# One-hot scatter on TensorE: a window of 12 destinations in groups of eight chunks, every source one-hot on VectorE

## The reference

```python
batch0 = jnp.zeros((512,), jnp.int32)
x = x + _L0_gnn_ref(_layernorm(x), batch0, edge_index, edge_attr_16, ...)[0]
x = x + _L0_ffn_ref(_layernorm(x)[None], ...)[0]
x = x + _L1_gnn_ref(_layernorm(x), edge_index, edge_weight, ...)
x = x + _L1_ffn_ref(_layernorm(x)[None], ...)[0]

# in _L0_gnn_ref: 32 graphs of 16 nodes, 8 heads, attention inside each graph
eb = edge_attr @ We + be
attn = attn.at[b_idx, loc_src, loc_dst].add(eb)     # a bias for each edge, summed where edges repeat
attn = jax.nn.softmax(attn, axis=2)
# in _L1_gnn_ref: Chebyshev terms over the weighted adjacency
deg = jax.ops.segment_sum(edge_weight, row, num_segments=n)
out = jax.ops.segment_sum(norm_w[:, None] * h[row], col, num_segments=n)
```

## Time and profile before

| | |
|---|---|
| median of 3 runs | 804.68 us (804.19 to 804.76) |
| the profiled execution | 805.79 us, its span from first to last instruction 804.0 us |
| busy: PE, PEld | 675.7 us (84%), 566.8 us (70%) |
| busy: DVE, ACT, POOL | 589.9 us (73%), 462.0 us (57%), 119.1 us (15%) |
| granted TensorE clock, mean | 0.93 |
| chain that ended last | PE 60%, DVE 20%, issue 7%, DMA 5% |

### The profile page before, as it was taken

How to read it: one execution, slowest core, us unless ns; L and a number is a source line. 1 busy time by engine, 2 the same in 40 slices (tenths; PEclk the granted TensorE clock), 3 DMA queues, 4 the chain that set the end, 5 groups by cost and what they waited for, 6 DMA issues and landing times.

```text
span 804.0 us, 23192 instructions
## 1 busy us (share of the span) xinstructions
PE 675.7 (84%) x8392; PEld 566.8 (70%) x8393; DVE 589.9 (73%) x1220; ACT 462.0 (57%) x804; POOL 119.1 (15%) x175
## 2 busy tenths in 40 slices
PE   2995888866659899999997099999669999999991
PEld 1454788854349899999987054444368999999991
DVE  4658988864469898888896673345578888888881
ACT  3360888862146687777765361111247888878780
POOL 2000000002000022112222200000000324433233
PEclk9897999996959999999999589999879999999996
DMA  9504000000105888989883850000117888889764
GB/s 305 213 1 158 0 0 0 0 1 1 67 3 192 300 280 270 327 285 339 288 265 86 264 197 2 1 0 1 69 58 246 262 256 269 257 269 281 254 199 86
DMA packets 37775, 127.67 MB, mean 159 GB/s; under 512 B 5441, under 2 KB 6033, under 8 KB 37569
## 3 DMA queue, kind: packets, MB, share of 16 engines
q1 hardware_dynamic: 31712, 119.39, 42.8%
q0 software_dynamic: 3648, 6.23, 5.3%
q10 hardware_dynamic: 2352, 1.23, 0.7%
HBM read 117.85 MB, written 10.03 MB: 159 GB/s over the span
## 4 chain that ended last, share of the span: by engine, by line
PE 60%; DVE 20%; issue 7%; DMA 5%; ACT 2%; POOL 2%; ACTq 1%; DVEq 1%; SPq 0%; POOLq 0%
PE pb L1473 11%; PE pb L1474 11%; PE pb L1475 11%; PE pb L1696 5%; DMA r_stage<-in_chunks 5%; PE pb L1572 4%; DVE r_split L952 4%; PE pb L1727 3%; PE pb L1729 3%; PE pb L1728 3%; DVE r_work L1073 2%; PE pb L1482 2%; ACT r_split L681 1%; PE pb L1570 1%; DVE r_work L1065 1%
## 5 line engine op out<-in xcount | busy, mean ns | idle before, releaser
L952 DVE SCALAR_TENSOR_TENSOR r_split<-r_stage,r_split 128x1024 f16<-128x1024 f32 (+1 forms) x160 | 230.3, 1443 | 47.3 <-ACT r_split L681 46.8
L681 ACT ACTIVATE r_split<-r_stage 128x1024 f16<-128x1024 f32 (+1 forms) x160 | 197.3, 1237 | 49.5 <-PE pb L1729 31.3
L1473 PE MATMUL pb<-r_work,r_split 128*128 128x160 f16 x864 | 184.0, 234 | 6.9 <-DVE r_work L1333 5.1
L1474 PE MATMUL pb<-r_work,r_split 128*128 128x160 f16 x864 | 184.0, 234 | 0.0
L1475 PE MATMUL pb<-r_work,r_split 128*128 128x160 f16 x864 | 184.0, 234 | 0.0
L1727 PE MATMUL pb<-r_work,r_split 128*128 128x160 f16 x608 | 129.9, 233 | 5.4 <-ACT r_work L779 3.2
L1729 PE MATMUL pb<-r_work,r_split 128*128 128x160 f16 x608 | 129.9, 233 | 0.0
L1728 PE MATMUL pb<-r_work,r_split 128*128 128x160 f16 x608 | 129.9, 233 | 0.0
L1570 PE MATMUL pb<-r_work 128*128 128x64 f16 x512 | 87.9, 195 | 11.6 <-DVE r_work L1073 11.6
L1473 PEld LDWEIGHTS pb<-r_work,r_split 128*128 128x128 f16 x864 | 84.9, 98 | 8.6 <-issue 7.1
L1572 PE MATMUL pb<-r_work 128*128 128x256 f16 x512 | 89.7, 276 | 0.0
(11 more groups left out here) (283 smaller groups left out, 1331.7 us busy)
## 6 DMA issues: line engine op xcount, KB each, us to landing
r_stage<-in_chunks SPq DMA_DIRECT2D x68, 768.0 KB, 5.2
r_stage<-in_chunks SPq DMA_DIRECT2D x92, 512.0 KB, 4.9
r_gnn<-in_cheb_lin SPq DMA_DIRECT2D x3, 1024.0 KB, 8.8
r_split<-in_cheb_lin SPq DMA_DIRECT2D x3, 1024.0 KB, 12.0
x_dram<-x_sb SPq DMA_DIRECT2D x10, 256.0 KB, 2.7
x_sb<-in_x SPq DMA_DIRECT2D x1, 1024.0 KB, 5.7
r_split<-in_Wq SPq DMA_DIRECT2D x1, 1024.0 KB, 9.8
r_work<-in_attr SPq DMA_DIRECT2D x1, 1024.0 KB, 11.2
```

What stands on the lines that cost most here:

```text
L681: nc.scalar.activation(x.hi(c), x.stage(c), ACT.Copy, scale=W_SCALE).then_inc(x.whi, 1)
L952: V.scalar_tensor_tensor(x.lo(c), x.stage(c), W_SCALE, x.hi(c), ALU.mult, ALU.subtract)\
L1473: MM(o, sh, mh, start=start, stop=False)
L1474: MM(o, sh, ml, start=False, stop=False)
```

## The change

The window falls from 64 to 12 destinations, and the edge bias uses the same window: one matmul of 2 x 12 x 8 = 192 columns, written at a register's column. The place in the graph of 16 is the destination's low four bits; a window that starts at place e covers places e to e + 11, past 15 too, so each tile block has a whole bank of two halves (high, low) of 256 columns, and the halves are folded afterwards by a reduction over the four groups of 128 columns. The second register of a chunk (`ends`) is the low bits of its first destination times 8. Buffers hold NC = 8 chunks instead of 4; the loop has 8 iterations of two buffers, and each buffer loads its own 8 + 8 registers. All source one-hots are made by DVE and none by ACT. The one-column closing matmuls take the place of the 512-column ones, over eight banks. Four reductions and one update replace the four updates behind the scatter. `weight_lo` of chunks 0 to 3 leaves its place ahead of the scores: two stand behind DVE's one-hots, two inside the attention loop, at t = 1 and t = 2. `dl_hot` is made in the wide path alone. The wide path keeps buffers of four.

```diff
-    W = 64
+    W = 12
-        score_m = [view(r_work, 8 + b, ...) for b in range(2)]
+        score_m = [view(r_work, 26 + b, ...) for b in range(2)]
+        NC = 8
...
-            V.tensor_scalar(src_neg[:, :], pb[0][:, 0:C], -1.0, None, ALU.mult)
             ch.link(V.tensor_scalar(w_lo[:, :], pb[0][:, 3 * P:3 * P + C], EDGE_SCALE, None, ALU.mult))
-            V.tensor_copy(base_i[:, :], pb[1][0:1, 0:C])
+            ch.link(V.tensor_copy(firsts_i[:, 0, :], pb[1][0:1, 0:C]))
+            ch.link(V.tensor_scalar(firsts_i[:, 1, :], firsts_i[:, 0, :], GN - 1, None, ALU.bitwise_and))
+            ch.link(V.tensor_scalar(firsts_i[:, 1, :], firsts_i[:, 1, :], float(H), None, ALU.mult))
...
-            for c in range(AHEAD):
-                weight_lo(ex[0], 0, c)
-
             dve.wait_ge(score_psum, T)
...
+            def hots_narrow(i, b, free):
+                if free:
+                    dve.wait_ge(hot_used, i * 2 + (b - 1))
+                at = bass.ds(i * (2 * NC) + b * NC, NC)
+                V.tensor_tensor(rel_hot[b], bc(iota_n[:, 0:W], 1, NC), bc(rel_h[:, at], 2, W), ALU.is_equal)\
+                    .then_inc(rel_ready, 1)
+                for c in range(NC):
+                    one = bass.ds(i * (2 * NC) + (b * NC + c), 1)
+                    V.tensor_scalar(src_hot_n[b][:, c, :], iota_n[:, :], src_f[:, one], None, ALU.is_equal)
+                dve.wait_ge(rel_ready, i * 2 + (b + 1))
+                for s, w in enumerate((w_h16, w_l16)):
+                    V.tensor_tensor(dst_n[b][:, :, s, :], rel_hot[b], bc(w[:, at], 2, W), ALU.mult)
+                for s, eb in enumerate((eb_hi, eb_lo)):
+                    last = V.tensor_tensor(ebd_n[b][:, :, s, :].rearrange("p c (g h) -> p c g h", h=H),
+                                           bc(rel_hot[b], 3, H), bc(eb[:, at, :], 2, W), ALU.mult)
+                last.then_inc(hot_ready, 1)
...
+            for c in range(2):
+                weight_lo(ex[0], 0, c)
             dve.wait_ge(scatter_psum, 1)
             flat = score.rearrange("p t k h -> p t (k h)")
-            for s in range(2):
-                for i in range(2):
-                    ins = V.scalar_tensor_tensor(...)
-                    ch.link(ins)
+            for t in range(T):
+                ch.link(V.tensor_reduce(eb_sum[:, t, :], pb[4 + t][:, :].rearrange("p (x q) -> p q x", x=4), AX_X,
+                                        ALU.add))
+            ch.link(V.scalar_tensor_tensor(flat, eb_sum, 1.0 / EB_SCALE, flat, ALU.mult, ALU.add))
...
                 if 1 <= t <= T:
                     head_lo(t - 1)
+                if 1 <= t <= 2:
+                    weight_lo(ex[0], 0, t + 1)
                 if t >= 2:
                     project(t - 2)
...
+            def scatter_narrow(i, b):
+                firsts, ends = [nc.values_load_multi_w_load_instructions(
+                    firsts_i[0:1, s, bass.ds(i * (2 * NC) + b * NC, NC)], engines=[mybir.EngineType.PE], min_val=0,
+                    max_val=top, skip_runtime_bounds_check_because=why)[1]
+                    for s, top, why in (...)]
                 pe.wait_ge(hot_ready, i * 2 + (b + 1))
-                pe.wait_ge(hot_act, i * (2 * AC) + (b + 1) * AC)
+                for c in range(NC):
+                    cols, near = bass.ds(firsts[c], W), bass.ds(ends[c], W * H)
+                    for t in range(T):
+                        w = src_hot_n[b][:, c, t * P:(t + 1) * P]
+                        MM(pb[t][:, cols], w, dst_n[b][:, c, 0, :], start=False, stop=False, skip_group_check=True)
+                        MM(pb[t][:, cols], w, dst_n[b][:, c, 1, :], start=False, stop=False, skip_group_check=True)
+                        last = MM(pb[4 + t][:, :].rearrange("p (s q) -> p s q", s=2)[:, :, near], w,
+                                  ebd_n[b][:, c, :, :], start=False, stop=False, skip_group_check=True)
+                last.then_inc(hot_used, 1)
...
-            for t in range(T + 2):
+            for t in range(2 * T):
                 MM(pb[t][:, :], zeros[:, :], iota_n[:, :], start=True, stop=False, skip_group_check=True)
...
-            for t in range(T + 2):
-                last = MM(pb[t][:, :], zeros[:, :], iota_n[:, :], start=False, stop=True, skip_group_check=True)
+            for t in range(2 * T):
+                last = MM(pb[t][:, 0:1], zeros[:, :], iota_n[:, 0:1], start=False, stop=True, skip_group_check=True)
```

More of the change, by code:

```diff
@@ L108, in build_network @@
         xn = view(r_work, 16, T * D, F32, "p (t d) -> p t d", t=T)
[L109 removed]
+        score_m = [view(r_work, 26 + b, T * H // 2 * GN, F32, "p (t h k) -> p t h k", t=T, h=H // 2) for b in range(2)]
         w_raw = [view(r_split, 8 * m, K * D, F32) for m in range(4)]
@@ L708, in _ @@
                 weight_hi(ex[0], 0, c)
[L710 to L731, removed]
             act.wait_ge(scatter_psum, 1)
@@ L1055, in one_hots @@
                 at = bass.ds(i * (2 * GC) + b * GC, GC)
[L1056 to L1059, removed]
+                for c in range(GC):
                     one = bass.ds(i * (2 * GC) + (b * GC + c), 1)
                     V.tensor_scalar(src_hot[b][:, c, :], iota_n[:, :], src_f[:, one], None, ALU.is_equal)
[L1062 to L1071, removed]
+                for c in range(GC):
+                    one = bass.ds(i * (2 * GC) + (b * GC + c), 1)
+                    for dst, w in ((dst_hi, w_hi), (dst_lo, w_lo)):
+                        V.tensor_scalar(dst[b][:, c, :], iota_n[:, :], dst_f[:, one], w[:, one], ALU.is_equal,
+                                        ALU.mult)
                 for s, eb in enumerate((eb_hi, eb_lo)):
@@ L1557, in _ @@
                 last.then_inc(score_psum, 1)
-            def scatter(i, b, windowed, firsts):
-                pe.wait_ge(hot_ready, i * 2 + (b + 1))
-                pe.wait_ge(hot_act, i * (2 * AC) + (b + 1) * AC)
+            def scatter_narrow(i, b):
+                firsts, ends = [nc.values_load_multi_w_load_instructions(
+                    firsts_i[0:1, s, bass.ds(i * (2 * NC) + b * NC, NC)], engines=[mybir.EngineType.PE], min_val=0,
+                    max_val=top, skip_runtime_bounds_check_because=why)[1]
+                    for s, top, why in ((0, N - W, "a minimum with N - W made them"),
+                                        (1, (GN - 1) * H, "the low bits of a number made them"))]
+                pe.wait_ge(hot_ready, i * 2 + (b + 1))
+                for c in range(NC):
[7 more added lines that the diff above has]
+                last.then_inc(hot_used, 1)
@@ L1563, in scatter, with scatter_wide @@
+            def scatter_wide(i, b):
+                pe.wait_ge(hot_ready, i * 2 + (b + 1))
                 for c in range(GC):
[L1564 to L1567, removed]
                     for t in range(T):
                         w = src_hot[b][:, c, t * P:(t + 1) * P]
[L1570 to L1574, removed]
@@ L1575, in scatter @@
-                last.then_inc(hot_used, 1)
[L1577 to L1582, removed]
-                            base_i[0:1, bass.ds(i * (2 * GC), 2 * GC)], engines=[mybir.EngineType.PE], min_val=0,
-                            max_val=N - W, skip_runtime_bounds_check_because="a minimum with N - W made them")[1]
+                        MM(pb[t][:, :], w, dst_hi[b][:, c, :], start=False, stop=False, skip_group_check=True)
@@ L1585, in all_scatter @@
+                        MM(pb[t][:, :], w, dst_lo[b][:, c, :], start=False, stop=False, skip_group_check=True)
+                        last = MM(pb[4 + t][:, :].rearrange("p (s q) -> p s q", s=2)[:, :, 0:P], w,
+                                  ebd[b][:, c, :, :], start=False, stop=False, skip_group_check=True)
+                last.then_inc(hot_used, 1)
+            def all_scatter(scatter, n):
+                with pe.Fori(0, C // (2 * n)) as i:
                     for b in range(2):
-                        scatter(i, b, windowed, firsts)
+                        scatter(i, b)
```

43 lines of the change are left out of this document (20 added, 23 removed).

## The result

The changed kernel takes 854.06 us (median of 4 runs, 851.89 to 854.99) against 804.43 us of the kernel before (4 runs, 801.65 to 804.76): a ratio of 1.062, 95% interval 1.059 to 1.065, some 49.6 us slower. Forecast were 838.5 us with a range of 826 to 855, and slower with 0.89. Sign and mechanism held. The profiled execution of after took 854.99 us, its span 853.2.

The account below looks back on a forecast made before the run. Bound before: PE and DVE alternating; after: PE's queue. Terms -2.7 + 33.4 - 0.6 + 1.7 + 1.7 = +33.5 against the median 804.7 gave about 838.2, with rounding 838.5 us, range 826 to 855.

Parts of the forecast that it names:

- What bounds the kernel: Scatter: before, PE and DVE alternating, 6.2 to 6.3 us per two buffers; after the change, PE's queue.
- The second address: PE's queue in the scatter: one more register operation per tile costs 0.087 us, making a tile 0.206 us.
- The loads: Scatter group heads: two register loads each, no longer hidden, 2.2 us for an iteration's first group and 1.65 for the second.
- DVE's one-hots: Scatter: eight chunks take DVE 4.4 us against 5.5 before, fitting in 8.5 us per group, so costing only before the first.
- The moved splits: Four weight splits leave DVE's queue ahead of the scores: scores start 4.3 us sooner, PE's scatter 2.7 with longer first one-hots.
- the third split: In attention, between the low part and the spread of block 2, on the path to PE: +1.7 us.
- The fourth: Weight split ahead of DVE's update, which waits for PE anyway: nothing, if PE's projection covers 1.7 us.
- The tail: Behind the scatter: one-column closing matmuls -0.6 us; four PSUM reductions and one update take 3.5 us, +1.7.
- (a): Rival, PE's queue: the second register operation costs only its 32 ns, tile 0.151 us, 810 us; chance 0.08.
- (b): Rival: PE's queue is not the bound, operation and loads hide, engines alternate as now, 781 us, faster; chance 0.09.
- (c): Rival: granted clock falls to half, array's tile 0.21 to 0.27 us, 838 to 841 us; no different outcome, no chance given.
- (d): Rival: narrow path not taken, two 512-column matmuls per tile, some +170 us; chance 0.03 together with code fetched anew.

Follow-up runs that it names:

- the last two kernels: Changed kernel with bias products at a fixed place, one register operation a tile, splits moved: four buffers of four chunks, 782.69 us; two of eight, 787.12 us.

## Why the prediction was right in sign and off in size

**What bounds the kernel** was read rightly for the change: PE's queue, with its heads on the path. Before, it wasn't the queue, since the kernel with nearly no register operations kept its time. That the alternation of the engines was the bound fits the last two kernels, which lose nearly all waits between PE and DVE and with them 13.6 and 12.5 us of the stage. It isn't shown by itself: both also lighten DVE's work per chunk and leave ACT out, and one halves the number of hand-offs. No run separates these.

**The second address** is the step that failed in size. The prediction divided the 0.119 us of a tile into 0.032 for three pairs and 0.087 for the operation, because a stream of pairs alone passes the queue at 11 ns each. That made two effects additive which overlap. With one pair, two or three behind it, the operation holds the queue for about 0.115 us; without the second matmul the scatter was not shorter by 0.1 us. With no pair between two operations, at the head of a group (L1555 and L1560, 108.779 and 108.874 us in after), they start 0.095 us apart. So the first pair behind an operation adds about 0.02 us, the second and third nothing. The true tile is 2 x 0.117 = 0.234, close to the upper bound of 0.238 that the prediction had named ("if it costs all the 0.119") and priced at 855. The mis-sized term is this operation per tile: 512 x 0.028 = 14 of the 15.6 us. The two numbers that I had, the pace of a stream with the operation and the pace of one without, can't tell an additive price from an overlapping one. I took the additive reading as if it were measured, when both ends were equally open.

**The loads** stand: heads of 2.15 and 1.61 us against 2.2 and 1.65. How a load's price grows with its registers wasn't known, and made no difference to the sum.

**DVE's one-hots**, 4.35 us against 4.4, hidden behind PE from the second group on, as said. **The moved splits**: the scores at 62.60 against 62.45, the first matmul at 70.92 against 70.9, so -2.6 against -2.7; the third split +1.67 against +1.7. That the first two agree to 0.1 us is in part luck: in the kernels whose code ahead of the scatter is nearly the same, the scores start anywhere from 61.2 to 62.8 us. The fourth, at 245.52 in after, isn't hidden quite: the update starts directly behind it, 0.59 us after PE's last projection matmul starts (246.60), where before it was 0.41 (201.37 and 201.78). That is 0.2 us and not nothing. The kernel with the moves alone bears their sum out: 2.6 us less than before, as expected, where the first buffer doesn't grow.

**The tail**: the reductions start 1.00 us after the last scatter matmul instead of 1.61, the forecast -0.6. The four from PSUM take 2.87 us, 0.70 each from start to start, and with the update the first maximum starts 3.63 us after the first of them, against 1.84 before: +1.8 for +1.7. The Trainium skill (SBUF — State Buffer, section "Door 1: The DMA port swizzle") gives PSUM lines of 8 bytes, and says of patterns that aren't contiguous there that they slow down matmuls. The prediction's estimate from it, that the stride would make each reduction as dear as the strided one in SBUF, 1.07 us, would have had 4.3 us here. The trace does not agree for these reads by DVE; a reduction of as many elements in SBUF took 1.07 again (at 223.66).

**The rivals.** (a), the operation at its own 32 ns, fell: the kernel before with a second register would then have kept its 804 us, and took 853. (b), a queue that isn't the bound, fell with it. (c), the clock, came about as described: the granted clock fell to 0.72, in one experiment to 0.50, and the stage didn't get longer: the queue's 0.234 us a tile is slower than the array's 0.213 at the lower level. (d), the wide path, did not come: the narrow lines ran 512 times.

Of the 49.6 us, the sum of terms as measured has 47.2 (scatter) - 2.6 - 0.6 + 1.8 + 1.7 = 47.5, and the layer norm starts 47.0 us late. The remaining 2 us lie behind the layer norm, where nothing was changed. From there to the end the profiled executions of the ten kernels here took anything from 583.1 us (four buffers) to 588.9 (after), with 586.8 before, so 2 us there tell nothing; what makes them differ stays open.

## What to carry to other kernels

A matmul at a register's address has a price in PE's queue that no busy time shows. Before a change adds a register operation to a stream of small matmuls, compare the queue's pace with the array's: so many operations a tile by 0.115 us against so many columns. While the first is smaller they are free (one a tile here), and beyond it they set the pace (two a tile). Here the narrower bias product saved the array 0.03 us a tile and cost the queue 0.115. Kept where it is free, the narrow window is part of the fastest kernel here, 782.69 us against 804.43; how much of that gain is the window's, the buffers' or the engines' new shares isn't separated.

And a caution for sums like mine: a price that is got by dividing one pace into parts is an assumption until a run takes one part away.

## What the runs showed of the hardware

- A register operation of 32 ns between matmuls holds PE's queue for about 0.115 us (0.117 in the mean of the 64 in a group), with one, two or three pairs of weight load and matmul behind it. A fused one of 37 ns (every fourth on these lines) is hardly dearer: at 108.874 in after the next operation starts 0.115 us behind it. Whether both addresses of a tile could be made by one such operation wasn't tried.
- A load of registers on PE's queue takes 0.49 us for one, 0.588 for eight and 1.105 for 16.
- The stage took the same 148.1 us at a mean granted clock of 0.72 and of 0.50 while the queue was the bound. A tile of the array's takes 0.133 us at the full level and 0.213 at the lower one.
